# Attention scores on TensorE: the fifth pass as pairs of 64-row matmuls, chunks of 400 keys

## The reference

```python
q = query @ w_q
k, v = jnp.split(context @ w_kv, 2, axis=-1)
scores = jnp.einsum('bhqd,bhkd->bhqk', q, k) * SCALE     # 16 heads of 64
attn = jax.nn.softmax(scores, axis=-1)
out = jnp.einsum('bhqk,bhkd->bhqd', attn, v)
```

## Time and profile before

| | before |
|---|---|
| median of the timed runs | 2590.8 us (2589.98 to 2591.02) |
| profiled execution: time, span | 2596.5 us, 2594.7 us |
| busy: TensorE, its weight loads | 2354.1 us, 2144.9 us |
| busy: VectorE, ScalarE, GpSimd | 1708.4, 1515.9, 1796.1 us |
| mean granted TensorE clock | 0.954 |

### The profile page before, as it was taken

How to read it: one execution, slowest core, us unless ns; L and a number is a source line. 1 busy time by engine, 2 the same in 40 slices (tenths; PEclk the granted TensorE clock), 3 DMA queues, 4 the chain that set the end, 5 groups by cost and what they waited for, 6 DMA issues and landing times. The chain is left out here.

```text
span 2594.7 us, 43059 instructions
## 1 busy us (share of the span) xinstructions
PE 2354.1 (91%) x13872; PEld 2144.9 (83%) x13872; DVE 1708.4 (66%) x2631; ACT 1515.9 (58%) x2456; POOL 1796.1 (69%) x906
## 2 busy tenths in 40 slices
PE   5948999999999999999999999999999947865777
PEld 3638999999999999999999999999999945744666
DVE  7746666666666666666666666666666625768772
ACT  4645666666666666666666666666666525443442
POOL 1015888888888888888888888888888637643453
PEclk9979999999999999999999999999999968976888
DMA  4777878887878888888877788888887558810000
GB/s 131 227 188 170 196 192 197 197 198 193 192 194 193 192 201 195 195 196 200 193 192 194 193 193 198 197 194 198 198 196 190 131 106 206 185 49 0 9 9 17
DMA packets 387682, 434.18 MB, mean 167 GB/s; under 512 B 45700, under 2 KB 362280, under 8 KB 387624
## 3 DMA queue, kind: packets, MB, share of 16 engines
q1 hardware_dynamic: 387624, 433.45, 68.6%
HBM read 162.73 MB, written 52.43 MB: 83 GB/s over the span
## 5 line engine op out<-in xcount | busy, mean ns | idle before, releaser
L505 POOL TENSOR_TENSOR p_pt_lo<-p_landed,p_pt_hi 128x768 fp32r<-128x768 f32 (+1 forms) x512 | 1005.3, 1986 | 359.6 <-ACT p_pt_hi L569 359.6
L741 PE MATMUL p_acc<-p_nat,p_pt_hi 128*128 128x384 f32 x3328 | 976.6, 361 | 13.6 <-POOL p_pt_lo L505 13.3
L743 PE MATMUL p_acc<-p_nat,p_pt_lo 128*128 128x192 f32 x3328 | 845.2, 254 | 0.0
L601 ACT ACTIVATE p_prob<-p_scores,p_negmax 128x800 f32<-128x800 f32 (+1 forms) x512 | 471.3, 926 | 515.6 <-DVE p_negmax L677 515.6
L725 PE MATMUL p_scores<-p_ct_hi,p_q_hi 128*128 128x512 f32 (+2 forms) x2048 | 711.3, 351 | 38.7 <-DVE p_ct_hi L701 27.3
L725 PE MATMUL p_scores<-p_ct_hi,p_q_lo 128*128 128x512 f32 (+2 forms) x2048 | 705.0, 347 | 0.0
L683 DVE STREAM_TRANSPOSE p_turned<-p_prob 128x1664 f32<-128x1664 f32 x256 | 489.3, 1911 | 317.0 <-ACT p_prob L601 317.0
L741 PEld LDWEIGHTS p_acc<-p_nat,p_pt_hi 128*128 128x128 f32 x3328 | 630.0, 189 | 15.3 <-issue 13.7
L743 PEld LDWEIGHTS p_acc<-p_nat,p_pt_lo 128*128 128x128 f32 x3328 | 640.0, 192 | 0.0
L569 ACT ACTIVATE p_pt_hi<-p_landed 128x768 fp32r<-128x768 f32 (+1 forms) x512 | 432.2, 892 | 156.7 <-PE p_acc L743 151.5
L725 PEld LDWEIGHTS p_scores<-p_ct_hi,p_q_hi 128*128 128x128 f32 x2048 | 388.8, 190 | 87.3 <-issue 28.0
(11 more groups left out here) (191 smaller groups left out, 2757.8 us busy)
## 6 DMA issues: line engine op xcount, KB each, us to landing
p_landed<-p_turned SPq DMA_DIRECT2D x2048, 104.0 KB, 2.2
p_raw<-in_ctx SPq DMA_DIRECT2D x96, 312.0 KB
o_scratch<-p_o_t SPq DMA_DIRECT2D x256, 96.0 KB, 2.7
qk_scratch<-p_out_a SPq DMA_DIRECT2D x16, 1024.0 KB, 4.6
p_oa<-o_scratch SPq DMA_DIRECT2D x32, 512.0 KB, 4.8
p_stage<-qk_scratch SPq DMA_DIRECT2D x31, 512.0 KB, 3.9
p_stage<-qk_scratch SPq DMA_DIRECT2D x62, 256.0 KB, 4.3
p_stage<-in_ctxT SPq DMA_DIRECT2D x31, 401.0 KB, 3.3
```

What stands on the lines that cost most here:

```text
L505: nc.gpsimd.tensor_tensor(pt_lo[:, t0:t1, :, :], by_tile(slot, t0, t1), bits(pt_hi[:, t0:t1, :, :]), ALU.subtract).then_inc(pt_lo_done, 1)
L601: nc.scalar.activation(prob[:, lo:hi], scores[:, S0 + lo:S0 + hi], ACT.Exp, bias=negmax[:, par:par + 1], accum_out=rowsum[:, par, h:h + 1] ...
L741: nc.tensor.matmul(acc[k % 2][:, 0:2 * DC], pt_hi[:, t, :, :].rearrange("p i x -> p (i x)"), x[:, t, :], start=t == 0, stop=False, skip_gr ...
L743: last = nc.tensor.matmul(acc[k % 2][:, 0:DC], pt_lo[:, t, :, :].rearrange("p i x -> p (i x)"), x[:, t, 0:DC], start=False, stop=t == KT - ...
```

## The change

In attend, the chunks become 400, 400, 400 and 402 keys, each at the end or the start of its own bank (PLACE), so that a half is contiguous still. Passes one to four stay matmuls with 128 rows. The fifth, low queries x high context of the block of 64, is made with 64 rows alone: the rows of q_lo and of the context that hold the high part. In chunks 1 and 3 the high part now lies in rows 64 to 127 and the low part in rows 0 to 63 (ROWS_B), so that the two matmuls of a half are on the upper and on the lower rows of the array. They are issued one behind the other, after the eight 128-row matmuls of the half, and write to two different banks. The product of two low parts, which the old fifth pass made as well, is left out. The low rows are subtracted chunk by chunk, four pieces a batch instead of two, and the counts of ct_b_done change with it.

```diff
-    CHALF = [(0, 802), (802, CW)]
-    EDGE = (CW - 2 * 512) // 4 * 2
-    CHUNKS = [(0, EDGE), (EDGE, EDGE + 512), (EDGE + 512, EDGE + 1024), (EDGE + 1024, CW)]
-    S0 = 512 - EDGE
-    MID = EDGE + 512
+    C = 400
+    CHUNKS = [(0, C), (C, 2 * C), (2 * C, 3 * C), (3 * C, CW)]
+    CHALF = [(0, 2 * C), (2 * C, CW)]
+    MID = 2 * C
+    PLACE = [512 - C, 512, 3 * 512 - C, 3 * 512]
+    UPPER, LOWER = slice(0, DCB), slice(DCB, P)
+    ROWS_B = [(UPPER, LOWER), (LOWER, UPPER)]
...
-                        sp.wait_ge(ct_b_done, n * 2 + 2)
+                        sp.wait_ge(ct_b_done, n * 4 + 4)
...
-                        sp.wait_ge(ct_b_done, n * 2 + 3)
+                        sp.wait_ge(ct_b_done, n * 4 + 6)
...
-                    dst = ct_hi[1 - par][DCB:P, 1, lo:hi]
-                    nc.gpsimd.tensor_tensor(dst, stage[DCB:P, u - 6, 0:hi - lo], bits(dst), ALU.subtract).then_inc(ct_b_done, 1)
-                    pool.wait_ge(ct_b_done, n * 2 + (u - 3))
+                    for c in (2 * (u - 6), 2 * (u - 6) + 1):
+                        (c0, c1), rows = CHUNKS[c], ROWS_B[c % 2][1]
+                        dst = ct_hi[1 - par][rows, 1, c0:c1]
+                        nc.gpsimd.tensor_tensor(dst, stage[rows, u - 6, c0 - lo:c1 - lo], bits(dst), ALU.subtract).then_inc(ct_b_done, 1)
+                    pool.wait_ge(ct_b_done, n * 4 + (2 * u - 6))
...
-            nc.vector.tensor_tensor(ct_hi[0][lower, 1, :], first_b[lower], bits(ct_hi[0][lower, 1, :]), ALU.subtract).then_inc(ct_b_done, 2)
+            for c, (c0, c1) in enumerate(CHUNKS):
+                dst = ct_hi[0][ROWS_B[c % 2][1], 1, c0:c1]
+                nc.vector.tensor_tensor(dst, first_b[ROWS_B[c % 2][1], c0:c1], bits(dst), ALU.subtract).then_inc(ct_b_done, 1)
...
-                for c, (lo, hi) in enumerate(CHUNKS):
-                    if c % 2 == 0 and not (first and j == 0):
-
-                        pe.wait_ge(exp_left if c == 0 else exp_done, s)
-                    ct_a, ct_b, ct_al = (t[:, lo:hi] for t in (ct_hi[par][:, 0, :], ct_hi[par][:, 1, :], ct_lo[par]))
-                    terms = ((q(q_hi, 0), ct_a), (q(q_lo, 0), ct_a), (q(q_hi, 0), ct_al), (q(q_hi, 1), ct_b), (q(q_lo, 1), ct_b))
-                    for m, (w, x) in enumerate(terms):
-                        last = nc.tensor.matmul(scores[:, S0 + lo:S0 + hi], w, x, start=m == 0, stop=m == len(terms) - 1)
-                    if c == 1:
-                        last.then_inc(left_ready, 1)
-                last.then_inc(scores_ready, 1)
+                for h in range(2):
+                    if not (first and j == 0):
+
+                        pe.wait_ge(exp_done if h else exp_left, s)
+                    for c in (2 * h, 2 * h + 1):
+                        lo, hi = CHUNKS[c]
+                        ct_a, ct_b, ct_al = (t[:, lo:hi] for t in (ct_hi[par][:, 0, :], ct_hi[par][:, 1, :], ct_lo[par]))
+                        terms = ((q(q_hi, 0), ct_a), (q(q_lo, 0), ct_a), (q(q_hi, 0), ct_al), (q(q_hi, 1), ct_b))
+                        for m, (w, x) in enumerate(terms):
+                            nc.tensor.matmul(scores[:, PLACE[c]:PLACE[c] + hi - lo], w, x, start=m == 0, stop=False)
+                    for c in (2 * h, 2 * h + 1):
+                        (lo, hi), rows = CHUNKS[c], ROWS_B[c % 2][0]
+                        last = nc.tensor.matmul(scores[:, PLACE[c]:PLACE[c] + hi - lo], q(q_lo, 1)[rows], ct_hi[par][rows, 1, lo:hi],
+                                                start=False, stop=True)
+                    last.then_inc(scores_ready if h else left_ready, 1)
```

More of the change, by code:

```diff
@@ L599, in step @@
                     act.wait_ge(turned_done, s)
-                for h, (lo, hi, done) in enumerate(((0, MID, exp_left), (MID, NKV, exp_done))):
-                    nc.scalar.activation(prob[:, lo:hi], scores[:, S0 + lo:S0 + hi], ACT.Exp, bias=negmax[:, par:par + 1],
+                for h, (lo, hi, at, done) in enumerate(((0, MID, PLACE[0], exp_left), (MID, NKV, PLACE[2], exp_done))):
+                    nc.scalar.activation(prob[:, lo:hi], scores[:, at:at + hi - lo], ACT.Exp, bias=negmax[:, par:par + 1],
                                          accum_out=rowsum[:, par, h:h + 1]).then_inc(done, 1)
@@ L671, in step @@
                 dve.wait_ge(left_ready, s + 1)
-                nc.vector.tensor_reduce(halfmax[:, par, 0:1], scores[:, S0:S0 + MID], AX.X, ALU.max, negate=True).then_inc(halfmax_done, 1)
+                nc.vector.tensor_reduce(halfmax[:, par, 0:1], scores[:, PLACE[0]:PLACE[0] + MID], AX.X, ALU.max, negate=True).then_inc(halfmax_done, 1)
                 dve.wait_ge(scores_ready, s + 1)
-                nc.vector.tensor_reduce(halfmax[:, par, 1:2], scores[:, S0 + MID:S0 + NKV], AX.X, ALU.max,
+                nc.vector.tensor_reduce(halfmax[:, par, 1:2], scores[:, PLACE[2]:PLACE[2] + NKV - MID], AX.X, ALU.max,
                                         negate=True).then_inc(halfmax_done, 1)
@@ L690, in body @@
                     step(r, j, first)
-            lower = slice(DCB, P)
             dve.wait_ge(ct_a_hi_done, 2)
@@ L715, in step_scores @@
                     pe.wait_ge(q_done, b * 2 + 2)
-                    pe.wait_ge(ct_b_done, b * 2 + 2)
+                    pe.wait_ge(ct_b_done, b * 4 + 4)
                 q = lambda t, k: t[par][:, k, (j % SB) * P:(j % SB + 1) * P]
-                for c, (lo, hi) in enumerate(CHUNKS):
-                    if c % 2 == 0 and not (first and j == 0):
-                        pe.wait_ge(exp_left if c == 0 else exp_done, s)
-                    ct_a, ct_b, ct_al = (t[:, lo:hi] for t in (ct_hi[par][:, 0, :], ct_hi[par][:, 1, :], ct_lo[par]))
-                    terms = ((q(q_hi, 0), ct_a), (q(q_lo, 0), ct_a), (q(q_hi, 0), ct_al), (q(q_hi, 1), ct_b), (q(q_lo, 1), ct_b))
-                    for m, (w, x) in enumerate(terms):
-                        last = nc.tensor.matmul(scores[:, S0 + lo:S0 + hi], w, x, start=m == 0, stop=m == len(terms) - 1)
-                    if c == 1:
-                        last.then_inc(left_ready, 1)
-                last.then_inc(scores_ready, 1)
+                for h in range(2):
[12 more added lines that the diff above has]
+                    last.then_inc(scores_ready if h else left_ready, 1)
             def product(r, j, first):
```

## The result

The changed kernel is slower: 2689.6 us (2686.3 to 2696.1, 4 runs) against 2590.9 (4 runs), a ratio of 1.0375 with an interval of 1.0356 to 1.0394, some 98 us. The forecast was 2752. The time lies between the bounds of 2680 and 2810, and nearest to the rival that had the pair last as long as one matmul (2696).

What follows compares the result with a forecast made beforehand. TensorE alone was taken as the bound. A half costs 0.39 + 0.184 + 0.11 - 0.369 = +0.315 us, 256 steps +161 us; with 0.5 more on the median, 2752 us, range 2680 to 2810.

Steps and rivals of the forecast that it cites:

- The bound: In attention's 256 steps TensorE alone is the limit, and any time added to it reaches the end in full.
- The trip: Going from 128-row to 64-row matmuls and back, twice a step: 0.39 us each, read from the bias matmul.
- 0.09 of hold: At each change of rows, the next weight load is held until 0.09 us after the stream before has ended.
- 0.11 of open load: At each change of rows, the weight load's own 0.11 us is not hidden behind a streaming matmul.
- The second matmul of the pair: The other 64-row matmul of a half: taken to add 0.11 us, between bounds of 0 and 0.38.
- The rest at nothing: Work outside the 64-row matmuls: +0.5 us for the first batch's VectorE pieces; GpSimd's added instructions covered by its waits.
- One matmul long: Rival for the pair: both loads and streams side by side, +0.205 us a half, 2696 us; chance 17%.
- One behind the other: Rival for the pair: the two streams don't overlap, +0.39 us a half, 2791 us; chance 20%.
- The free switch: Rival: changing to 64 rows costs nothing, so the kernel gets faster, 2522 us; chance 9%.
- the room of the loop: In the ScalarE, GpSimd, product loop: 0.27 us a step before the seventh tile, limiting a gain to 69 us.

Runs made afterwards that it cites:

- e2: The changed kernel with rows not swapped, so both 64-row matmuls of a half use the upper rows: 2785.2 us, 1.0738 of the kernel before.
- e4: The changed kernel with each 64-row matmul alone behind its own chunk's four 128-row matmuls, four trips a step, no pair: 2990.9 us, 1.1527 of before.
- e7: The changed kernel with each pair of 64-row matmuls issued twice in the same trip: 2782.6 us, 1.073 of the kernel before.
- e5: The changed kernel with the fifth pass left out and all other work kept: 2558.8 us, 0.986 of the kernel before.
- e1: The changed kernel with its chunks, PSUM places, swapped rows and four subtractions, but the fifth pass on 128 rows again: 1.000 of the kernel before.
- e3: The changed kernel with both pairs behind all sixteen 128-row matmuls, one trip into 64 rows a step instead of two: 1.0036 of the kernel before.
- e6: The changed kernel with the fifth pass on rows 0 to 95 and the high part in rows 0 to 63 in all chunks: 0.9999 of before.

## Why the prediction was right, and where it missed

*The bound.* Right: TensorE alone, before and after, and what e2, e4 and e7 added to its time came out in full. The other way it holds for 36 us only (e5).

*The trip.* Right in size and in kind. The 0.39 us read from one bias matmul was 0.38 around the pair and 0.387 as the mean over 1024 trips in e4. The 0.09 of hold and 0.11 of open load are in the rows after as they were in those of before. The Trainium skill, "TensorEngine Tiling (Array Packing)", Key Properties, says that a change of tiling mode drains the engine; by that rule e4 had to be the worst of these kernels, and it was, by some 300 us over the change.

*The second matmul of the pair.* This is the term that was mis-sized. The step took 0.11 between bounds of 0 and 0.38, with the argument that loads come one after the other in every row. All those rows were loads into the same rows of the array. On the same 64 rows the second load of a pair starts 0.11 us behind the first (e2), on different ones 3 ns (the change): the term should have been nothing. 0.11 x 512 is 56 of the 62 us by which the forecast was too high. The page "TensorE: Matmul & The Clock Gate" of the Trainium skill, Part 3, gives about 4 ns between the starts of packed matmuls; by that figure the estimate was 2698, and the trace agrees with its 3 to 4 ns. The bound from below was there, and I weighed a row of another kind of case above it. The forecast had 0.43 for a mechanism that did not come, and the time lies between the bounds because they took in the rival that did, with its 0.17: 161 us of loss were forecast and 98 measured.

*The rest at nothing.* Right: e1. The four pieces of VectorE at the start took 0.57 us each where one had taken 1.82, 0.46 us more in sum, as forecast. GpSimd's pieces of 400 take 893 ns; its busy time rose by 9 us, and it waits for ScalarE 441.4 us in all instead of 359.6. None of this reached the end beyond the 3 us that e1 can tell.

*The rivals.* One matmul long was what happened. One behind the other is e2, 2785 where the rival had 2791. The free switch was not so for 64 rows, though the 64-column form that spoke for it behaved as read. Its price was too high, however: it had 69 us for the room of the loop, and e5 leaves 36. The sum took the whole 0.27 us from the end of GpSimd's work to the start of the seventh tile as room. In e5 0.05 of it stay between the end of GpSimd's row (1002.04 + 2.12) and the load at 1004.21, and the load that waits is in the open and puts the next matmul 0.09 later (0.29 instead of 0.20). The 0.13 that are left, times 256, are 33 us.

## What to carry to other kernels

Price a change of the array's shape by the trip and not by the matmul: here 0.39 us for going from 128-row to 64-row matmuls and back. A pair saves half of its columns (0.184 us at 2 x 400), so by these numbers two pairs of such a size in one trip come out about even (e3, 9 us over), and a gain needs more, which no run had. Before making one engine's pass cheaper, take the pass out altogether for one run: if that gives 36 us where the engine's own time says 189, the loop behind it is the next bound and limits what a cheaper pass can bring.

The experiments don't point to a kernel that beats the one before. One trip a step (e3) comes out at 1.0036, and one trip in two steps would need the scores of two steps in PSUM, eight banks beside the two of the product. That wasn't tried.

## What the runs showed of the hardware

- Two 64-row matmuls of float32r on the upper and lower rows, with outputs in different banks, start together with their loads (3 or 4 ns apart in 512 pairs), and a second pair costs 0.18 us at 400 columns, with its loads hidden (e7). Whether the different banks are needed was not varied.
- On the same 64 rows the second load starts 0.11 us behind the first, and the second stream takes its full 0.18 us more (e2).
- 96 rows of weights are as free as 128 (e6, 0.9999); 64 rows are held on both sides, 0.09 us of hold and 0.11 of open load on each side, with one matmul (e4), two, or four (e3, e7).
- What the hold waits for is only argued. It starts 0.09 us after the stream before has ended, whether that had 256 columns or 400, which fits an array that has to be empty; no run varied that by itself.
